# Layer-0 linear attention of a four-layer kernel: two groups in lockstep against a staggered pipeline of single groups

## The reference

```
q = LN(x) Wq + bq;  k = ctx Wk + bk;  v = ctx Wv + bv      (LN without gain and bias)
q = elu(q) + 1;  k = elu(k) + 1
S = k^T q  per head and sequence (8 x 8)
out = (v S) / (sum over channels of q*k + 1e-6)
x = x + out Wo + bo
```

## Time and profile before

| | |
|---|---|
| median of 3 runs | 3828.25 us (3825.55 to 3829.85) |
| the profiled execution | 3834.41 us, its span 3832.2 us |
| mean granted clock of TensorE | 0.841 |
| instructions | 67502 |
| TensorE products busy | 2824.3 us, 74% |
| VectorE busy | 2417.4 us, 63% |
| ScalarE busy | 1053.2 us, 27% |
| GpSimd busy | 586.9 us, 15% |

### The profile page before, as it was taken

One profiled execution on the slowest core, in us unless ns is written; L12 is line 12 of the kernel. 1 busy time (PEld: TensorE's weight loads), 2 busy tenths in 40 slices (PEclk: granted clock), 3 DMA queues, 4 the chain that ended last, 5 costly groups with the idle time before them and its releaser, 6 DMA issues. The chain is left out here.

```text
span 3832.2 us, 67502 instructions
## 1 busy us (share of the span) xinstructions
PE 2824.3 (74%) x24301; PEld 1938.4 (51%) x24346; DVE 2417.4 (63%) x5789; ACT 1053.2 (27%) x1472; POOL 586.9 (15%) x1034
## 2 busy tenths in 40 slices
PE   5885333999599999999986677769890465887247
PEld 3553222666366656666545555547570354665126
DVE  4446997899445555555544478877302556888768
ACT  1122333777100000000002234445330111444230
POOL 0001222000000000000000034324216001443003
PEclk8675555999799999999997788889995677999569
DMA  2001001111221221212200000000131221000001
GB/s 71 11 16 53 0 0 26 26 26 22 89 89 56 78 89 44 88 55 77 88 7 23 17 3 0 0 22 28 48 92 44 54 57 27 1 0 6 0 0 44
DMA packets 119501, 141.53 MB, mean 37 GB/s; under 512 B 75732, under 2 KB 87508, under 8 KB 118360
## 3 DMA queue, kind: packets, MB, share of 16 engines
q1 hardware_dynamic: 111864, 119.66, 10.0%
q0 software_dynamic: 7520, 20.34, 1.8%
HBM read 122.66 MB, written 17.30 MB: 37 GB/s over the span
## 5 line engine op out<-in xcount | busy, mean ns | idle before, releaser
L1310 PE MATMUL banks<-l1f_xe,l1f_w 128*128 128x512 f32 x1024 | 486.7, 598 | 10.3 <-DVE l1f_xe L1509 10.3
L1509 DVE TENSOR_TENSOR l1f_xe<-l1f_hT,l1f_rwb 128x512 f32<-128x512 f32 x256 | 173.5, 693 | 299.8 <-PE banks L1312 277.6
L1312 PEld LDWEIGHTS banks<-l1f_w,l1f_xe 128*128 128x128 f32 x2048 | 269.2, 192 | 123.6 <-issue 123.6
L1515 DVE TENSOR_TENSOR l1f_ae<-l1f_aoT,l1f_rwb 128x512 f32<-128x512 f32 x256 | 172.7, 690 | 160.3 <-PE banks L1340 156.1
L1312 PE MATMUL banks<-l1f_w,l1f_xe 128*128 128x128 f32 x2048 | 269.9, 275 | 0.0
L1310 PEld LDWEIGHTS banks<-l1f_xe,l1f_w 128*128 128x128 f32 x1024 | 176.8, 192 | 141.0 <-issue 126.8
L1340 PE MATMUL banks<-l1f_ae,l1f_w 128*128 128x512 f32 x512 | 225.3, 599 | 1.4 <-DVE l1f_ae L1515 1.4
L214 POOL COPY x<-xn 128x512 f32 (+1 forms) x32 | 19.5, 610 | 987.6 <-DVE xn L1539 972.1
L223 PE MATMUL banks<-consts,l3p_h 128*128 128x128 f32 x64 | 17.3, 424 | 200.1 <-DVE l3p_h L140 200.1
L1340 PEld LDWEIGHTS banks<-l1f_ae,l1f_w 128*128 128x128 f32 x512 | 97.1, 192 | 118.3 <-issue 116.1
L535 PE MATMUL banks<-identb,l0f_q 128*128 128x128 bf16 x256 | 30.2, 312 | 129.5 <-DVE l0f_q L459 129.5
(11 more groups left out here) (466 smaller groups left out, 6843.0 us busy)
## 6 DMA issues: line engine op xcount, KB each, us to landing
l1f_rwb<-l1f_shares SPq DMA_DIRECT2D x128, 512.0 KB, 4.2
l1a_ctx<-in_ctxT SPq DMA_DIRECT2D x32, 256.0 KB, 3.7
l3p_ctx<-in_ctxT SPq DMA_DIRECT2D x32, 256.0 KB, 3.9
l0a_ctxT<-in_ctxT SPq DMA_DIRECT2D x16, 256.0 KB, 2.8
l2f_sent<-l0f_zero SPq DMA_DIRECT2D x4, 1024.0 KB, 9.2
l2p_ctxT<-in_ctxT SPq DMA_DIRECT2D x16, 256.0 KB, 2.7
l2e_rows<-l2f_sent SPq DMA_DIRECT2D x16, 256.0 KB, 2.9
l2f_answers<-l2e_y POOLq DMA_DIRECT2D x16, 256.0 KB, 2.7
```

Of the source, the lines that this page charges most:

```text
L1310: pe.matmul(bank, w[:, n, e, :], xe[:, e % NB, :], start=(e == 0), stop=(e == E - 1))
L1312: last = pe.matmul(v_bank[:, D * j:D * j + D], xe[:, e % NB, P * j:P * j + P], w[:, 2, e, :], start=(e == 0 and j == 0), stop=(e == E - 1) ...
L1509: dve.tensor_tensor(xe[:, e % NB, :], hT[:, m, :], rwb[:, m, e, :], ALU.mult).then_inc(s.xe_ready, 1)
L1515: dve.tensor_tensor(ae[:, e % NB, :], aoT[:, m, :], rwb[:, m, e, :], ALU.mult).then_inc(s.ae_ready, 1)
```

## The change

The stage is rewritten; the rest of the kernel stays.

- In place of two lanes with their own halves of everything there is one set of buffers and one role for each PSUM bank: `turn_bank` for both sets of transposes, `k_bank`, `v_bank`, `q_bank`, two `kq_banks`, `o_bank`, `y_bank`. Only the context has two buffers.
- Each engine runs `pipeline` over 16 single groups, with lags 0 to 3, so that up to four groups are under way.
- The norm moves from VectorE to ScalarE: Identity with per-token scale `rstd` and bias `shift` = -mean * rstd, computed once at the start of the stage. It stands behind the query features in ScalarE's list.
- The three fp32 bias products of one row become one bf16 product each of 96 rows: the bias is split into three bf16 parts that add up to it exactly, each part in a row of its own (rows 0, 32 and 64 of `rows`, the others zero), against bf16 ones, repeated four times by the operand's stride. The split takes place on VectorE at the start of the stage, and TensorE waits for it (`bias_ready`). One load of 128 x 384 replaces three rows.
- VectorE adds y to `k.x` in place; GpSimd copies only the statistics.

```diff
-            def steps(i):
-                for u in range(LANES):
-                    wait(sp, s.v_psum, LANES * i)
-                    sp.dma_start(ctxT[:, u, :], d["ctxT"][:, bass.ds((LANES * i + u) * GT, GT)]).then_inc(s.ctx_loaded, 16)
+            def load(g, m):
+                wait(sp, s.v_psum, g - 1)
+                wait(sp, s.ctx_loaded, 16 * g)
+                sp.dma_start(ctxT[:, m, :], d["ctxT"][:, bass.ds(g * GT, GT)]).then_inc(s.ctx_loaded, 16)
...
+            def bias_rows(bank, n):
+                pe.matmul(bank, onesb[0:96, :], rows[0:96, D * n:D * n + D].unsqueeze(1).to_broadcast([96, TG, D]), start=True,
+                          stop=False, skip_group_check=True)
+            def turn(g, m):
+                pe.wait_ge(s.h_ready, g + 1)
+                wait(pe, s.oT_ready, g - 1)
+                four_transposes(pe, k, turn_bank, h).then_inc(s.hT_psum, 1)
+            def outer(g, m):
+                pe.wait_ge(s.qk_ready, g + 1)
+                wait(pe, s.kq_ready, g)
...
+            def project(g, m):
+                pe.wait_ge(s.oT_ready, g + 1)
+                wait(pe, s.xn_ready, g)
+                bias_rows(y_bank, 2)
...
+            def keys(g, m):
+                pe.wait_ge(s.ctx_loaded, 16 * (g + 1))
+                wait(pe, s.k_ready, g)
+                bias_rows(k_bank, 1)
...
+            def queries(g, m):
+                pe.wait_ge(s.hT_ready, g + 1)
+                wait(pe, s.q_ready, g)
+                bias_rows(q_bank, 0)
...
+            def weigh(g, m):
+                pe.wait_ge(s.kq_ready, g + 1)
+                pe.wait_ge(s.vT_ready, g + 1)
+                wait(pe, s.o_ready, g)
...
+            def turn_o(g, m):
+                pe.wait_ge(s.o_ready, g + 1)
+                pe.wait_ge(s.hT_ready, upto(g + 2, k.NG))
+                four_transposes(pe, k, turn_bank, o).then_inc(s.oT_psum, 1)
+            pipeline(pe, k.NG, [(1, turn), (2, outer), (3, project), (1, keys), (1, queries), (2, weigh), (1, values), (2, turn_o)])
...
+            def norm(g, m):
+                wait(act, s.hT_psum, g)
+                settle(act, k)
+                for j in range(TG):
+                    t = TG * g + j
+                    last = act.activation(h[:, j, :], k.x[:, bass.ds(t, 1), :], ACT.Identity, bias=shift[:, bass.ds(t, 1)],
+                                          scale=k.rstd[:, bass.ds(t, 1)])
+                last.then_inc(s.h_ready, 1)
...
+            pipeline(act, k.NG, [(1, copy_hT), (1, features_k), (1, features_q), (0, norm), (1, copy_vT), (2, copy_oT)])
...
+            def copy_mv(g, m):
+                pool.wait_ge(s.stats_ready, g + 1)
+                settle(pool, k)
+                pool.tensor_copy(k.mv[:, bass.ds(TG * g, TG), :], k.mvn[:, 0]).then_inc(s.mv_copied, 1)
+            pipeline(pool, k.NG, [(3, copy_mv)])
...
+            dve.scalar_tensor_tensor(out=shift[:, :], in0=k.mv[:, :, 0], scalar=-1.0, in1=k.rstd[:, :], op0=ALU.mult, op1=ALU.mult)\
+                .then_inc(s.shift_ready, 1)
+            chain.did(dve.memset(rows[:, :], 0.0))
+            chain.did(dve.tensor_copy(onesb[:, :], k.ones))
+            dve.wait_ge(s.weights, WEIGHTS)
+            go(dve.tensor_copy(part[:, 0, :], bias[:, :]))
+            go(dve.tensor_tensor(rest[:, :], bias[:, :], part[:, 0, :], ALU.subtract))
+            go(dve.tensor_copy(part[:, 1, :], rest[:, :]))
+            go(dve.tensor_tensor(rest[:, :], rest[:, :], part[:, 1, :], ALU.subtract))
+            go(dve.tensor_copy(part[:, 2, :], rest[:, :]))
+            for n in range(3):
+                last = dve.tensor_copy(rows[32 * n:32 * n + 1, :], part[32 * n:32 * n + 1, n, :])
+            last.then_inc(s.bias_ready, 1)
...
+                dve.tensor_tensor(x, x, y_bank.rearrange("p (t c) -> p t c", c=D), ALU.add).then_inc(s.xn_ready, 1)
+                dve.wait_ge(s.xn_ready, g + 1)
+                settle(dve, k)
+                for n in range(TG):
+                    chain.did(dve.bn_stats(k.bn6[:, 0, n, :], k.x[:, bass.ds(TG * g + n, 1), :]))
...
+            pipeline(dve, k.NG, [(2, mask), (3, new_x), (2, divide), (1, features)])
```

More of the change, by code:

```diff
@@ L274, in sb @@
             return ctx.enter_context(nc.sbuf_tensor(f"l0a_{name}", shape, dt))
-        s = sems(nc, ctx, "l0a", "var_ready std_ready rstd_ready weights ctx_loaded h_ready hT_psum hT_ready q_psum k_psum v_psum "
-                 "feat_exp vT_ready qk_ready kq_psum kq_ready o_psum o_ready oT_psum oT_ready y_psum xn_ready stats_ready x_done chain act_chain")
+        s = sems(nc, ctx, "l0a", "var_ready std_ready rstd_ready shift_ready weights split bias_ready ctx_loaded h_ready hT_psum hT_ready "
+                 "k_psum k_ready q_psum q_ready v_psum vT_ready qk_ready den_chain den_ready kq_psum kq_ready o_psum o_ready oT_psum "
+                 "oT_ready y_psum xn_ready stats_chain stats_ready mv_copied")
         w = sb("w", [P, 4, D])
-        wrow = sb("wrow", [1, 3, GT])
-        bv = sb("bv", [P, 1])
[L281 to L293, removed]
+        bias = sb("bias", [P, 3 * D])
+        rest = sb("rest", [P, 3 * D])
+        part = sb("part", [P, 3, 3 * D], BF16)
+        rows = sb("rows", [P, 3 * D], BF16)
+        onesb = sb("ones", [P, P], BF16)
+        bv = sb("bv", [P, 1])
+        shift = sb("shift", [P, k.NT])
+        ctxT = sb("ctxT", [P, 2, GT])
+        h = sb("h", [P, TG, D])
+        hT = sb("hT", [P, GT])
+        e = sb("e", [P, 2, GT])
+        r = sb("r", [P, 2, GT])
+        qk = sb("qk", [P, 2, TG, D])
+        prod = sb("prod", [P, TG, D])
+        den = sb("den", [P, TG * H])
+        vT = sb("vT", [P, GT])
+        kq = sb("kq", [P, SG, D])
+        o = sb("o", [P, TG, D])
+        oT = sb("oT", [P, GT])
+        turn_bank, k_bank, v_bank, q_bank = k.psum[0:4]
+        kq_banks, o_bank, y_bank = k.psum[4:6], k.psum[6], k.psum[7]
+        WEIGHTS = 16 * 6
         block = ctx.enter_context(nc.Block())
@@ L308, in _ @@
-            rounds(sp, k.NG // LANES, steps)
+            def load(g, m):
+                wait(sp, s.v_psum, g - 1)
+                wait(sp, s.ctx_loaded, 16 * g)
+                sp.dma_start(ctxT[:, m, :], d["ctxT"][:, bass.ds(g * GT, GT)]).then_inc(s.ctx_loaded, 16)
+            pipeline(sp, k.NG, [(0, load)])
         @block.tensor
         def _(pe):
[L312 to L361, removed]
@@ new lines, in weigh, with values @@
+            def weigh(g, m):
+                pe.wait_ge(s.kq_ready, g + 1)
+                pe.wait_ge(s.vT_ready, g + 1)
+                wait(pe, s.o_ready, g)
+                for q in range(SG):
+                    lo = S * (q % 2)
+                    last = pe.matmul(o_bank[lo:lo + S, D * (q // 2):D * (q // 2) + D], vT[:, S * q:S * q + S], kq[:, q, :],
+                                     start=True, stop=True)
+                last.then_inc(s.o_psum, 1)
+            def values(g, m):
+                wait(pe, s.vT_ready, g)
+                pe.matmul(v_bank, w[:, 2, :], ctxT[:, m, :], start=True, stop=True).then_inc(s.v_psum, 1)
@@ L371, in _ @@
             finish_stats_act(act, k, s)
[L372 to L392, removed]
@@ L394, in _ @@
-            rounds(act, k.NG // LANES, steps)
+            act.wait_ge(s.shift_ready, 1)
+            act.wait_ge(s.weights, WEIGHTS)
+            def norm(g, m):
+                wait(act, s.hT_psum, g)
+                settle(act, k)
+                for j in range(TG):
+                    t = TG * g + j
+                    last = act.activation(h[:, j, :], k.x[:, bass.ds(t, 1), :], ACT.Identity, bias=shift[:, bass.ds(t, 1)],
+                                          scale=k.rstd[:, bass.ds(t, 1)])
+                last.then_inc(s.h_ready, 1)
@@ new lines, in copy_hT, with features_k, features_q @@
+            def copy_hT(g, m):
+                act.wait_ge(s.hT_psum, g + 1)
+                wait(act, s.q_psum, g)
+                act.copy(hT[:, :], turn_bank).then_inc(s.hT_ready, 1)
+            def features_k(g, m):
+                act.wait_ge(s.k_psum, g + 1)
+                wait(act, s.qk_ready, g)
+                act.activation(e[:, 1, :], k_bank, ACT.Exp)
+                act.activation(r[:, 1, :], k_bank, ACT.Relu).then_inc(s.k_ready, 1)
+            def features_q(g, m):
+                act.wait_ge(s.q_psum, g + 1)
+                act.activation(e[:, 0, :], q_bank, ACT.Exp)
+                act.activation(r[:, 0, :], q_bank, ACT.Relu).then_inc(s.q_ready, 1)
@@ new lines, in copy_vT, with copy_oT @@
+            def copy_vT(g, m):
+                act.wait_ge(s.v_psum, g + 1)
+                wait(act, s.o_psum, g)
+                act.activation(vT[:, :], v_bank, ACT.Identity, bias=bv[:, 0:1]).then_inc(s.vT_ready, 1)
+            def copy_oT(g, m):
+                act.wait_ge(s.oT_psum, g + 1)
+                wait(act, s.y_psum, g)
+                act.copy(oT[:, :], turn_bank).then_inc(s.oT_ready, 1)
```

(22 more changed lines are left out.)

94 lines of the change are left out of this document (48 added, 46 removed).

## The result

The changed kernel takes **3688.4 us** (median of 4 executions) against 3827.6 for the kernel before, measured beside it: a ratio of **0.9635**, 95% interval 0.9616 to 0.9654. The forecast was 3705 (3683 to 3748). One of the four executions took 11115 us; it is not in the ratio, and without it the median is 3688.2. The medians differ by 139 us, the two profiled executions by 147, chiefly because the profiled execution of the old kernel was 7 us longer than its median. The profiled execution took 3686.95 us, its span 3685.4.

What follows compares the result with a forecast made beforehand. Layer-0 attention was bound by lockstep waits, a low TensorE clock and dear bias products. Start 6 + 16 x 10.4 + end 9 = 181 us instead of 304, 123 less: 3705 us, range 3683 to 3748.

Steps and rivals of the forecast that it cites:

- Only this stage changes: All-engine barriers fence the stages, so only layer-0 attention changes, from 304 to 181 us; later stages stay as long.
- Start: At the stage's start TensorE waits for the split of the biases (3.4 us) and begins 6 us in.
- The ring: Per-group loop of waits: TensorE 5.84 us, ScalarE 3.9, plus hand-overs 0.1, giving 9.8 us at 2.4 GHz.
- 3 x 0.26 + 4 x 1.1: TensorE's bias products (0.26 us each) and four product sets (1.1 each); with transposes 0.66, 5.84 us per group.
- The norm: Four norm activations on ScalarE, inside the per-group loop of waits: 1.5 us, bounds 1.1 to 2.2.
- Engine sums: Work per group: TensorE 8.55 us at 2.4 GHz, VectorE 7.5, ScalarE 5.6; GpSimd and SP worth 0.
- One sign: Expected in the stage's profile: VectorE waiting for the query features; no size given.
- The clock: TensorE's clock in the stage: 15% of the time at 1.2 GHz, mean 0.92, making the group period 10.4 us.
- P: Period from group to group in the stage: 9.8 us at 2.4 GHz, 10.4 with the low-clock share.
- 1.9 to 2.0: Microseconds a TensorE product set takes at 1.2 GHz, set against 1.16 at 2.4 GHz.
- The rival from the Trainium skill: Stage's clock stays lower, as short idles make it swing: at half the time low, stage 207 us, 3731; 17%.
- The better rival: ScalarE's norm slides into idle time and the clock holds: period 8.55 to 9.3, stage 152 to 164, 3676 to 3688; 11%.

Runs made afterwards that it cites:

- the early norm: Changed kernel with the norm before the key features in ScalarE's list: stage 155.7 us, period 8.55 us, time 3691.6 us (6 runs).
- the one with 96 rows: Kernel before, still lockstep, with fp32 bias products of 96 rows (95 of zeros) in place of one: stage 266.8 us, time 3802.2 us.

## Why the prediction was right, and where it was off

- **Only this stage changes.** 307.1 to 160.5 us, what comes behind it 3497.2 and 3496.8: right.
- **Start.** TensorE began at 35.84 us; I said 36. The split took 3.15 us (32.60 to 35.75), said 3.4.
- **The ring.** Right in every member, and the early norm confirms it. Its length was 9.8, measured 8.97 us. The term that was mis-sized is "3 x 0.26 + 4 x 1.1": outer and the three sets with their biases last 4.53 us, not 5.18. I added the bias product to a set of 1.1, where 0.9 is what a set takes once its first weights are loaded beside the bias product. The old kernel could not show it, its biases having one row.
- **The norm.** 1.64 us for four against 1.5. On the path it counts 1.54, from its start to the next copy's. The Trainium skill's figure (ScalarE: Activation LUTs, What ACT_TABLE_LOAD costs), from which I had estimated 1.64, fits to the hundredth.
- **Engine sums.** VectorE 117.5/16 = 7.3 (said 7.5), ScalarE 86.9/16 = 5.4 (5.6). GpSimd and SP: nothing on the path. TensorE busy 85% in steady running (said 85 to 90), its wait 1.2 to 1.3 us a step (1.2). One sign did not come: VectorE waits for the weighed values, 1.0 us a step, and not for the query features.
- **The clock.** I took 15% at 1.2 GHz; it was none after the start. From this 0.6 us of P, 10 of the 23 us by which the stage was shorter than said (181 against 158); the sets with biases make most of the others, 0.65 x 16 = 10 us. On the cause I was right in part: waits bring the clock down, and the one-row products prolong it in the old kernel, for some 20 to 40 us of its stage; why they did not in the pipeline is open. The 15% had no row of this stage behind it. (The 1.16 us that I set against "1.9 to 2.0" is a length, the others mostly distances; like for like it is 1.16 against 2.08.)
- **The rival from the Trainium skill** (TensorE: Matmul & The Clock Gate, A second HAM failure mode: psum-queue depth-cycling): short idles make the clock swing and cost throughput. A wait of 1.3 us in every 9 did not, in 110 us of steady running. In the lockstep kernels short waits did: after two of 1.0 and 2.2 us between the outer products the old kernel's set at 93.84 us takes 2.08 us, and the one with 96 rows falls at its waits of 1.4 and 2.2 us as well as at those of 3.7; there the rule holds. What matters between 1.3 us in nine and these was not tried.
- **The better rival** (P 8.55 to 9.3, stage 152 to 164, 11%) has the right size, 3688 at its edge, and half of its reason: the clock held. The other half, the norm sliding into idle time, did not come; that needed an edit of the order, and then gave 8.55. Forecast and better rival thus lie close: the errors of the forecast, 10 us each, both made it too long, and the measured time fell near the fast end of its range.
- **Where the gain comes from.** Bias products alone in the old lockstep: 66 us. Pipeline and the norm's move with one-row fp32 biases: 97. Both 147, so 16 us are shared.

## What to carry to other kernels

Draw each loop of waits through a single buffer, member by member, and also the one that comes second: here it was 0.4 us behind the first, and took most of what the first fix was worth. An engine with much idle time is still a bad home for work if the order puts it inside the loop; placed in the engine's own wait it was off the ring. A product of one row was dear here in three ways: its columns, a held-back weight load, and, in the kernel with waits, more time at 1.2 GHz. Rows of zeros took away the second and shortened the third.

## What the runs showed of the hardware that was not expected

- Weight loads run ahead past a product of 96 rows and not past one of 1 or 32 rows: 0.26 us per bf16 product, 0.32 per fp32 one (11.94 against 10.98 for three). The Trainium skill (TensorE: Matmul & The Clock Gate, Part 3, The mechanism) says in its list of what overlaps that weight loads run beside products in flight only where their row groups differ, and above it also allows a load into a background weight buffer. The 96-row product and the 128-row load share rows and overlap all the same, so against the list the measurement decides; that the product of 32 rows is not passed is said by neither. Why was not tried, nor any number of rows between 32 and 96.
- TensorE at 1.2 GHz streamed for twenty microseconds without rising (145 to 169 us of the old kernel) while a part of its products had one row, and rose within six when these had 96. The same old kernel also rose within nine microseconds in its second round, and seven of its falls came with no wait in nearly nine microseconds before; what decides is not known.
- fp32 against bf16 for the same 96 x 512 product: 0.67 us each ((10.98 - 8.97)/3).
